# Causal attention and a binarized feed-forward: turning tiles with VectorE squares and DMA stripes in place of TensorE

## The reference, cut to what matters

```python
q, k, v = x @ wq, x @ wk, x @ wv          # per batch: 1024 x 128
q, k = rope(q), rope(k)                   # turns the first 64 of the 128 numbers
s = (q @ k.T) / 128 - 1e30 * causal_mask  # 1024 x 1024
x1 = layernorm(x + softmax(s) @ v @ wo)
bw = lambda w: mean(abs(w), axis=1) * sign(w)
h = gelu(x1 @ bw(w1).T + b1)              # 512 wide
out = layernorm(x1 + h @ bw(w2).T + b2)
```

## Time and profile before

| | us |
|---|---|
| median of 3 runs (lowest, highest) | 344.56 (342.98, 345.43) |
| the profiled execution, its own time | 340.74 |
| its span, which the rows below divide | 338.9 |
| TensorE / VectorE / ScalarE / GpSimd busy | 300.7 / 268.0 / 200.2 / 139.8 |
| granted TensorE clock, share of full | 0.985 |
| packets of the 16 DMA engines, bytes | 26451, 14.67 MB |

### The profile page before, as it was taken

One profiled execution on the slowest core, in us unless ns is written; L12 is line 12 of the kernel. 1 busy time (PEld: TensorE's weight loads), 2 busy tenths in 40 slices (PEclk: granted clock), 3 DMA queues, 4 the chain that ended last, 5 costly groups with the idle time before them and its releaser, 6 DMA issues.

```text
span 338.9 us, 5451 instructions
## 1 busy us (share of the span) xinstructions
PE 300.7 (89%) x1739; PEld 234.6 (69%) x1739; DVE 268.0 (79%) x637; ACT 200.2 (59%) x362; POOL 139.8 (41%) x183
## 2 busy tenths in 40 slices
PE   3689799999999999998999999999999999885760
PEld 3567657875888677975888677966898587643540
DVE  2777637788578869888887968987888968889995
ACT  2256535795468745795378637793479556821533
POOL 1300301348033763158324753358324743095342
PEclk9999999999999999999999999999999999999896
DMA  7502001200040004200140005000210004000204
GB/s 234 168 2 62 1 3 57 66 2 0 5 121 3 1 0 127 61 2 1 51 137 0 0 0 166 20 0 0 84 40 0 2 0 126 1 0 0 64 0 125
DMA packets 26451, 14.67 MB, mean 43 GB/s; under 512 B 832, under 2 KB 25920, under 8 KB 26432
## 3 DMA queue, kind: packets, MB, share of 16 engines
...
...
## 4 chain that ended last, share of the span: by engine, by line
PE 55%; DVE 16%; ACT 13%; issue 8%; POOL 3%; DMA 2%; DVEq 0%; POOLq 0%; ACTq 0%
PE wide L413 13%; PE acc L454 8%; PE turn L440 6%; PE acc L462 4%; DVE hid_hi L1098 4%; ACT hid L822 3%; PE acc L512 3%; PE acc L511 3%; PE wide L499 3%; PE wide L501 2%; PE wide L500 2%; DVE qkT_lo L1089 2%; ACT L822 2%; PE turn L471 2%; ACT qkT_hi L816 2%
## 5 line engine op out<-in xcount | busy, mean ns | idle before, releaser
L806 ACT ACTIVATE prob<-wide,negmax 128x128 f32<-128x128 f32 (+3 forms) x64 | 47.3, 743 | 51.2 <-DVE negmax L1084 50.9
L308 POOL TENSOR_TENSOR hid_lo<-hid,hid_hi 128x1024 fp32r<-128x1024 f32 x26 | 61.6, 2371 | 27.1 <-DVE hid_hi L1098 27.1
L1084 DVE TENSOR_REDUCE negmax<-wide 128x1 f32<-128x128 f32 (+3 forms) x64 | 47.2, 750 | 28.7 <-PE wide L416 28.4
L454 PE MATMUL acc<-probT,xa 128*128 128x512 f32 (+3 forms) x176 | 66.7, 495 | 0.1
L300 POOL TENSOR_TENSOR qk_tok<-rot_cos,rot_sin 128x512 f32<-128x512 f32 x16 | 20.7, 1291 | 80.5 <-DVE rot_sin L1111 80.5
L413 PE MATMUL wide<-qkT_hi 128*128 128x512 f32 (+2 forms) x96 | 43.3, 451 | 6.2 <-ACT prob L806 6.0
L812 ACT ACTIVATE probT<-turn 128x512 f32<-128x512 f32 (+1 forms) x64 | 31.3, 515 | 24.3 <-PE turn L440 23.4
L440 PE MATMUL turn<-ident,prob 128*128 128x128 f32 x288 | 42.3, 274 | 1.8 <-DVE x1T_lo L1089 0.8
L1098 DVE CAST hid_hi<-hid 128x1024 fp32r<-128x1024 f32 x27 | 37.6, 1400 | 1.4 <-ACT hid L822 1.4
L454 PEld LDWEIGHTS acc<-probT,xa 128*128 128x128 f32 x176 | 29.8, 192 | 12.0 <-issue 10.5
L440 PEld LDWEIGHTS turn<-ident,prob 128*128 128x128 f32 x288 | 32.9, 141 | 7.2 <-issue 3.4
...
## 6 DMA issues: line engine op xcount, KB each, us to landing
...
w_sb<-in_L_ffn_w_dram SPq DMA_DIRECT2D x2, 256.0 KB, 5.2
out_dram<-y_out SPq DMA_DIRECT2D x2, 256.0 KB, 2.5
out_dram<-x SPq DMA_DIRECT2D x2, 256.0 KB, 3.0
```

The costliest lines, as they stand in the source:

```text
L308: pool.tensor_tensor(hid_lo[:, j, :], hid[:, j, :], hid_hi[:, j, :].bitcast(F32), ALU.subtract).then_inc(s_hid_lo, 1)
L454: ins = pe.matmul(acc[g][:, lo:BANK], xa[:, j, :], probT[g][:, j, lo:BANK], start=j == 0, stop=j == KEYS[g] - 1)
L806: act.activation(prob[:, ROW[r]:ROW[r + 1]], wide[r % 2][:, 0:(r + 1) * P], ACT.Exp, bias=negmax[:, r:r + 1], accum_out=rowsum[:, r:r + 1] ...
L1084: dve.tensor_reduce(negmax[:, r:r + 1], wide[r % 2][:, 0:(r + 1) * P], axis=AX.X, op=ALU.max, negate=True).then_inc(s_max, 1)
```

## The change

All engines' lists are new, written out for every step, with no loop and no separate tails: a step now holds x's turning and the first quarter of the projections of batch b, the rest of the projections and score rows 0 to 4 of b-1, score rows 5 to 7 and the weighing of b-2, the feed-forward of b-3 and b-4, the last norm of b-5 (on SP the numbering differs: `carry` of batch c comes in its step c+3).

1. Turning of the probabilities. `turn_prob`, `probT_out`, `probT_copy` go. `turn_row(r)` on VectorE transposes a whole row of `prob` within 32x32 squares, SBUF to SBUF, into `turned`. `carry` moves the squares to their places with 16 DMAs for rows 0 to 4 and 16 for rows 5 to 7, each from 32 partitions to 32 partitions in pieces of 32 numbers (128 bytes): 15 or 21 tiles x 32 partitions = 480 or 672 pieces. Counted over a batch: 18432 pieces. SP issues them all and waits for `s_turned` and, for the batch before, `s_px` first.
2. Turning of x. `turn_x` goes; `xq` is loaded as 32x32 squares by 4 DMAs of 1024 pieces of 128 bytes (`stripes`), and two VectorE transposes (`x_squares`) give `xT`. Its high part is still ScalarE's, its low part now GpSimd's.
3. Weighing. The projection makes q, k and x wvo together (384 columns, `project`); `weigh(r)` is row tile r: r+1 float32 products of 128x128x128 with `probT` stationary. `px_out` and `project_out` go.
4. ScalarE: `tok_copy` copies all 384 columns of two tiles at once in place of `skipped`; it takes over `hidden_high`.
5. GpSimd: takes `xT_low` and `second_norm`; first norm factors are made in halves; the sum of the rotation is in quarters.
6. PSUM: three pairs in turn for scores, projections and `up`, two banks in turn for the rest; each new user waits for the reader of the buffer's last user.

```diff
+            def stripes(c):
+                sp.wait_ge(s_xT[0], c)
+                sp.wait_ge(s_xT[1], c)
+                for n in range(NB):
+                    sp.dma_start(xq[n * BLK:(n + 1) * BLK, :].rearrange("j (m i) -> j m i", i=BLK),
+                                 x[c].rearrange("(m j) d -> j m d", j=BLK)[:, :, n * BLK:(n + 1) * BLK]
+                                 ).then_inc(s_xq_in, 16)
+            def carry(g, c):
+                rows = GROUPS[g]
+                sp.wait_ge(s_turned[rows[-1]], c + 1)
+                if c > 0:
+                    sp.wait_ge(s_px[rows[-1]], c)
+                span = slice(ROW[rows[0]], ROW[rows[-1] + 1])
+                for n in range(NB):
+                    squares = turned[n * BLK:(n + 1) * BLK, span].rearrange("i (m c j) -> i m c j", c=NB, j=BLK)
+                    for k in range(NB):
+                        keys = probT[k * BLK:(k + 1) * BLK, span].rearrange("i (m n j) -> i m n j", n=NB, j=BLK)
+                        sp.dma_start(keys[:, :, n, :], squares[:, :, k, :]).then_inc(s_probT_in[g], 16)
+                if live(b - 3):          # SP's step
+                    carry(0, b - 3)
+                    carry(1, b - 3)
+                if live(b - 6):
+                    store(b - 6)
+                if 0 < b < B:
+                    stripes(b)
+                if live(b - 2):
+                    tokens(b - 2)
...
+            def second_norm(h, c):       # GpSimd
...
+                for t in tiles(h):
+                    ins = pool.tensor_scalar(y_out[:, t, :], res2[:, t, :], ln2[:, 2, t:t + 1], ln2[:, 7, t:t + 1],
+                                             ALU.subtract, ALU.mult)
+            def step(b):                 # GpSimd's list
+                hidden_low(3, b - 4); xT_low(1, b - 1); first_factors(1, b - 3); second_factors(b - 5)
+                second_norm(0, b - 5); second_norm(1, b - 5); rotation_sum(0 to 2, b - 1); hidden_low(0, b - 3)
+                rotation_sum(3, b - 1); hidden_low(1, b - 3); first_factors(0, b - 2); xT_low(0, b); hidden_low(2, b - 3)
...
+            def weigh(r, c):             # TensorE
+                for g in range(len(GROUPS)):
+                    if r == GROUPS[g][0]:
+                        pe.wait_ge(s_probT_in[g], GROUP_IN * (c + 1))
+                dst = next_bank("px", r, c)
+                for j in range(r + 1):
+                    keys = slice(ROW[r] + j * P, ROW[r] + (j + 1) * P)
+                    ins = pe.matmul(dst[:, 0:D], probT[:, keys], tok[c % 2][:, j, 2 * D:QKV], start=j == 0, stop=j == r)
+                ins.then_inc(s_px[r], 1)
+            def step(b):                 # TensorE's list
+                project(1, b - 1); down(1, b - 4); up(0, b - 3); turn_y(0, b - 4); turn_y(1, b - 4)
+                project(2, b - 1); project(3, b - 1); weigh(0, b - 2); turn_qk(0, b - 1); up(1, b - 3); up(2, b - 3)
+                weigh(1, b - 2); weigh(2, b - 2); turn_qk(1, b - 1); up(3, b - 3); weigh(3, b - 2); turn_qk(2, b - 1)
+                scores(0, b - 1); weigh(4, b - 2); scores(1, b - 1); turn_qk(3, b - 1); scores(2, b - 1)
+                weigh(5, b - 2); weigh(6, b - 2); scores(3, b - 1); scores(4, b - 1); turn_x1(0, b - 2); weigh(7, b - 2)
+                scores(5, b - 1); project(0, b); scores(6, b - 1); down(0, b - 3); scores(7, b - 1); turn_x1(1, b - 2)
...
+            def turn_row(r, c):          # VectorE
+                dve.wait_ge(s_exp[r], c + 1)
+                for g in range(len(GROUPS)):
+                    if c > 0 and r == GROUPS[g][0]:
+                        dve.wait_ge(s_probT_in[g], GROUP_IN * c)
+                dve.transpose(turned[:, ROW[r]:ROW[r + 1]], prob[r % 3][:, 0:(r + 1) * P]).then_inc(s_turned[r], 1)
+            def x_squares(h, c):
+                if h == 0:
+                    dve.wait_ge(s_xq_in, 16 * NB * (c + 1))
+                if c > 0:
+                    dve.wait_ge(s_xT_lo[h], c)
+                dve.transpose(xT[:, half(h)], xq[:, half(h)]).then_inc(s_xT[h], 1)
+            def step(b):                 # VectorE's list
+                turn_row(3, b - 2); residual1(7, b - 3); turn_row(4, b - 2); statistics1(7, b - 3); x1T_low(0, b - 3)
+                row_max(5, b - 2); rotate(0, b - 1); row_max(6, b - 2); first_norm(1, b - 3); turn_row(5, b - 2)
+                row_max(7, b - 2); x1T_low(1, b - 3); rotate(1, b - 1); turn_row(6, b - 2); turn_row(7, b - 2)
+                reciprocals(0, b - 2); residual2(0 and 1, b - 4); rotate(2, b - 1); x_squares(0, b); residual1(0, b - 2)
+                rotate(3, b - 1); qkT_low(0, b - 1); statistics1(0, b - 2); x_squares(1, b); residual1(1 and 2, b - 2)
+                statistics2(0, b - 4); qkT_low(1, b - 1); statistics2(1, b - 4); residual1(3, b - 2); statistics1(1 and 2, b - 2)
+                reciprocals(1, b - 2); row_max(0, b - 1); statistics1(3, b - 2); qkT_low(2, b - 1); residual1(4, b - 2)
+                row_max(1, b - 1); qkT_low(3, b - 1); statistics1(4, b - 2); first_norm(0, b - 2); row_max(2, b - 1)
+                residual1(5 and 6, b - 2); turn_row(0, b - 1); row_max(3, b - 1); turn_row(1, b - 1); row_max(4, b - 1)
+                turn_row(2, b - 1); statistics1(5 and 6, b - 2)
...
+            def step(b):                 # ScalarE's list
+                exponentials(5, b - 2); tok_copy(0, b - 1); y_half(0, b - 4); exponentials(6, b - 2); x1T_high(1, b - 3)
+                exponentials(7, b - 2); y_half(1, b - 4); tok_copy(1, b - 1); gelu(0, b - 3); tok_copy(2, b - 1)
+                qkT_high(0, b - 1); hidden_high(0, b - 3); tok_copy(3, b - 1); gelu(1, b - 3); qkT_high(1, b - 1)
+                hidden_high(1, b - 3); gelu(2, b - 3); qkT_high(2, b - 1); gelu(3, b - 3); xT_high(0, b)
+                qkT_high(3, b - 1); exponentials(0, b - 1); hidden_high(2, b - 3); exponentials(1, b - 1)
+                hidden_high(3, b - 3); exponentials(2 to 4, b - 1); xT_high(1, b); x1T_high(0, b - 2)
```

More of the change, by code:

```diff
@@ L109, in attention_ffn_kernel @@
         rinv = sb("rinv", [P, NT])
-        prob = sb("prob", [P, ROW[NT]])
-        probT = [sb(f"probT{g}", [P, KEYS[g], BANK]) for g in range(NG)]
-        pxT = sb("pxT", [P, NG, BANK])
+        prob = [sb(f"prob{i}", [P, n * P]) for i, n in enumerate((7, 8, 6))]
+        turned = sb("turned", [P, ROW[NT]])
+        probT = sb("probT", [P, ROW[NT]])
         res1 = sb("res1", [P, NT, D])
@@ L228, in _ @@
-            run_steps(sp, step)
-            sp.wait_ge(s_y, at(1, end2, 1))
-            sp.dma_start(out[B - 3].rearrange("(n p) d -> p n d", p=P), y_out[:, :, :]).then_inc(s_stored, 16)
-            for c, y, done, before in ((B - 2, y_out, s_y, B - 2), (B - 1, y_last, s_y_last, 0)):
-                for h in range(NG):
-                    sp.wait_ge(done, before + h + 1)
-                    sp.dma_start(out[c][halves(h), :].rearrange("(n p) d -> p n d", p=P),
-                                 y[:, TG * h:TG * (h + 1), :]).then_inc(s_stored, 16)
@@ new lines, in store @@
+            def store(c):
+                sp.wait_ge(s_y, c + 1)
+                sp.dma_start(out[c].rearrange("(n p) d -> p n d", p=P), y_out[:, :, :]).then_inc(s_stored, 16)
+            def step(b):
+                if live(b - 3):
[7 more added lines that the diff above has]
+                    tokens(b - 2)
@@ L239, in _ @@
+            for b in range(B + 6):
+                step(b)
+            sp.wait_ge(s_stored, 16 * B)
         @block.gpsimd
@@ L356, in _ @@
+            for b in range(B + 5):
+                step(b)
         @block.tensor
         def _(pe):
[L358 to L371 removed]
+            pe.wait_ge(s_const, 7)
@@ L714, in down_prev, with turn_x1, up @@
+            def turn_x1(h, c):
+                pe.wait_ge(s_x1[h], c + 1)
+                dst = next_bank("x1T", h, c)
+                for t in range(TG):
+                    ins = pe.transpose(dst[:, t * P:(t + 1) * P], x1[c % 2][:, TG * h + t, :], ident[:, :])
+                ins.then_inc(s_x1T[h], 1)
+            def up(j, c):
+                if c == 0 and j == 0:
+                    pe.wait_ge(s_weights, 1)
                 if j == 0:
-                    pe.wait_ge(s_res1, at(NT, end, TG))
@@ L779, in _ @@
[L779 to L792 removed]
+                    ins = pe.transpose(dst[:, t * P:(t + 1) * P], yT[:, me], ident[:, :])
@@ new lines, in hidden_high, with y_half @@
+            def hidden_high(j, c):
+                act.wait_ge(s_gelu[j], c + 1)
+                if c > 0:
+                    act.wait_ge(s_down[NG - 1], c)
+                act.activation(hid_hi[:, j, :], hid[:, j, :], ACT.Copy).then_inc(s_hid_hi[j], 1)
+            def y_half(h, c):
+                act.wait_ge(s_down[h], c + 1)
+                if c > 0:
+                    act.wait_ge(s_yTok[h], c)
+                act.activation(yT[:, half(h)], bank_of["down", h, c][:, :], ACT.Identity, bias=b2_sb[:, 0:1],
+                               scale=alpha2[:, 0:1]).then_inc(s_yT[h], 1)
@@ L1429, in rotation_tables @@
```

(2 more changed lines are left out.)

1630 lines of the change are left out of this document (569 added, 1061 removed).

## The result

The changed kernel takes 367.44 us (median of 4 executions, 364.64 to 369.12); the kernel before, on the same chip, 344.02 (342.98 to 345.43). The ratio is 1.072, its 95% interval 1.066 to 1.078. The forecast was 324, with a range of 308 to 365. The profiled execution took 369.12 us; its span is 367.5, 1.6 less.

A forecast was written before the change was run, and what follows sets the result against it. TensorE bounds it: 36.3 of a 37.4 us step before, 30 to 31 after. Way in 45 + 7 x 33 + way out 43 = span 319, + 1.8 + 3.6 = 324 us; range 308 to 365.

The forecast's parts named there:

- TensorE, transposes, projection: TensorE's work a step: transposes and `project_out` removed, 6.7 us, wider projection added, 1.3; from 36.3 to 30 to 31.
- VectorE without the lock: VectorE's work a step before any waiting for GpSimd: from 31.5 to 28.3 us, including 5.9 for turning `prob`.
- Rival 1: VectorE's square transposes share GpSimd's lock: step 37 to 38 us, span 354, time 359; chance 0.12.
- GpSimd: GpSimd's work a step rises from 18.4 to 27.6 us, with norm factors 8.9 and `second_norm` 3.6.
- The packet: DMA transport in `carry`: a 128-byte packet takes 12 to 13 ns, so rows 5 to 7 take 8.7 us.
- Rival 2: In the carries, a packet costs 25 ns or more, or 32 partitions are served worse: step 39 to 41, time 380; chance 0.15.
- The cost of an issue: On SP's queue, one DMA costs 0.48 us to issue: 7.7 for the 16 of one `carry`, 18 us a batch.
- the circle: `weigh(5)` through scores, turning of row 7 and `carry(1)` to the next `weigh(5)`: 18.3 + 10.7 = 29.0 us, taken as hidden.
- The lock: VectorE's `first_norm` waits while GpSimd works, up to 2.4 us for each of two groups: 1 to 3 us a step.
- Way in: Start to `weigh(5)` of batch 0: first row maximum at 19.3, rows 0 to 7 some 15, carry 10.7; 45 us.
- Way out: From `weigh(5)` of batch 7 to the end: weighing, norms, feed-forward, store and hops sum to 43 us.
- Rival 3: Lists mesh badly, GpSimd's factors late for `first_norm(0)`, which precedes `row_max(2)` and turning: step 35.5, time 342; chance 0.17.

The follow-up runs named there:

- e1: Changed kernel with GpSimd waiting for `first_norm(0)` before `xT_low` and `hidden_low(2)`, no work moved: 347.75 us, ratio 1.017 to the kernel before.
- e13: e1 with first x loaded ahead of tables, last batch's `hidden_low` on VectorE, and `second_norm` on VectorE for the last three batches: 333.41 us, ratio 0.977.
- e7: e1 with only every second square's DMA issued, about half of the probabilities uncarried: 338.69 us, ratio 0.990 to the kernel before.
- e14: Changed kernel with only every second square's DMA issued, half of the probabilities uncarried, lock left in: 361.72 us, ratio 1.059 to the kernel before.
- e6: e1 with all 32 DMAs a batch, each carrying about half of its pieces: 345.32 us, ratio 1.008 to the kernel before.
- e4: Changed kernel with `second_norm` on ScalarE at its step's start and `second_factors` at the start of GpSimd's: 348.35 us, ratio 1.016 to the kernel before.
- e8: e1 and e4 together, with rotation tables and feed-forward weights loaded only once the first batch's x has landed: 352.63 us.

## Why the prediction was wrong

Its steps, in its order:

- **TensorE, transposes, projection.** TensorE's busy time is 31.6 in e1 and e13, where it doesn't overlap with stalls; 30 to 31 was forecast. Right within 1 us; the weighing's products take 0.24 (13 in 3.17 us), not 0.22.
- **VectorE without the lock**, 28.3: 28.1 in e1. The turning 5.9 a batch: 6.0. Rival 1 is out: GpSimd was at work beside 26 of the 64 turnings, and none is held up (the eight widest take 1.20 at most).
- **ScalarE** 26.7: 25.7. **GpSimd** 27.6: 28.8 busy in a round of the circle. `second_norm` was taken at 0.45 an instruction, inside a bound of 0.2 to 0.5, and takes 0.80, outside it: 6.3 a batch, not 3.6. The norm factors are under their 8.9, at 7.6 busy, which hides half of that. The line through the earlier trace rows came from tensor-to-tensor operations without per-partition operands.
- **The packet.** 12 to 13 ns; 13.9 for a packet of 128 bytes, 15.3 in the mean of all, the large ones included. Rival 2 is out in its premise. Its sign was there all the same: TensorE stands before `weigh(5)` with a DMA as releaser in five of the eight batches, for 0.6 to 3.9 us. It is the serial issues, not the packets: with half of the issues it doesn't stand at all (e7, e14). By the rule of the Trainium skill that was weighed there (page "DMA: Bandwidth & Descriptors", section "Specifications") 25 ns or more was at stake; no such price shows between SBUF tiles.
- **The cost of an issue.** 0.48 us, read from plain loads. A `carry`'s DMA takes 0.67 to 0.70 from start to start, whatever it carries (e6). The two carries together take 22 to 24 us, and `carry(1)` can't start before `carry(0)`'s issues are through. The prediction set 7.7 of issue against 8.7 of transport and left `carry(0)` out of the circle. In e1 `turned` of row 7 comes 18.9 us after `weigh(5)`, where 18.3 was forecast; `carry(0)`'s issues end 1.7 us later, and `carry(1)` takes 12.7 us from there to `weigh(5)`, not 10.7: 33.3, not 29.0. This error fell within the forecast of 33, which had 2 us of slack put on for other reasons; that was luck.
- **The lock: the step that failed.** "`first_norm` is SBUF to SBUF too and now meets a busier GpSimd; it may wait up to 2.4 us for each of its two groups: 1 to 3 us. VectorE: 29 to 31." The mechanism is right, and is the one showed. The size is 5.1 us, since four instructions meet three of GpSimd's in a row, and since the meeting isn't by chance: one event releases both engines. And it was booked as VectorE's load, which has room, where it stands on a circle through GpSimd. With the prediction's own prices that circle would be 38.1 - 5.1 - 2.7 = 30.3, or 31 to 33 with its 1 to 3 us of lock: within the forecast of 33. With the measured ones it is 38. Two of the 38 of the round above are TensorE's half clock, a term that the prediction didn't have. e1 takes away the lock and brings 20 us, 18 of them in the steps. e4 takes away the second term and, by that, part of the lock, and brings 19; in the profiled executions 12 are in the steps and 8 in the way out. e14 shows that the carries have no part in it.
- **Way in**, 45: 56.9. 7.1 of these 11.9 us are there at the first row maximum, which stands at 26.4, not 19.3; with x ahead of the tables it is 23.6 (e8). Another 4 are the serial carries: the 32 issues of batch 0 stand from 32.4 to 55.2 in SP's queue, and with half of them `weigh(5)` of batch 0 starts at 52.7 (e14).
- **Way out**, 43: 58.8. The chain was written down for batch 7 alone. GpSimd's list has batch 5's `second_norm` ahead of batch 7's `hidden_low`, and batch 6's ahead of batch 7's residual, 6.3 each. With these and batch 7's `hidden_low` on VectorE it is 42.2 (e13). That is the sum's 43, but with two of its terms made cheaper (`second_norm` 2.1, not 3.6, and `hidden_low`), so it doesn't test the sum as it was.

Rival 3 named the place (`first_norm(0)` ahead of `row_max(2)` and all turning) and GpSimd as the late one, but looked for it in the wait for the factors, which is 0.45 us; its 35.5 us a step was 1 short, and it had no error in the tail. So the steps missed for a lock of twice its price and a `second_norm` of nearly twice its price, in a circle through GpSimd that nobody had added up; the way out missed for the same engine's list, and the way in for other reasons. e13, which mends the first two, has `weigh(5)` of batch 0 at 53.6, steps of 33.4 and a way out of 42.2: nearly all of the 9 us by which it still misses 324 are in the way in.
